# A layernorm, attention and mixture-of-experts layer on eight cores: resident Q/K weights with single buffers, in place of streamed Q/K weights with double buffers

## The chip, the cores and the metric

The kernel runs on all 8 cores of one Trainium2 chip (trn2). Every core runs the same program on its own share of the tokens, and no core talks to another. The time is the device time of the slowest core, in microseconds (us). Five engines work side by side in a core, each in the order of its own queue: PE (TensorE, matmuls and transposes), DVE (VectorE), ACT (ScalarE), POOL (GpSimd) and SP (SyncE). In this kernel POOL and SP do little but issue DMAs.

## The reference, cut to what matters

```python
x: (4, 8192, 1024) float32                     # each core: 4096 tokens = 2 segments of 2048
xn = layernorm(x)                              # no scale, no shift
# attention on every 4th token of a 2048-token segment: 512 tokens, 16 heads of 64, causal
xi = xn.reshape(4, 4, 2048, 1024)[:, :, 0::4, :]
q, k, v = split(xi @ w_in.T + b_in, 3)         # w_in (3072, 1024)
p = softmax(where(causal, q @ k.T / 8, -1e9));  o = (p @ v) @ w_out.T + b_out
attn = zeros_like(xn);  attn[:, :, 0::4, :] = o
# feed-forward on every token
shared = (silu(xn @ ws1) * (xn @ ws2)) @ ws3   # inner width 256
g = top-6-of-8 of softmax(xn @ wr), renormalised
routed = sum_e g[e] * ((silu(xn @ w1[e]) * (xn @ w2[e])) @ w3[e])   # inner width 128
out = x + attn + shared + routed
```

## The kernel before, in words

A core's 4096 tokens are two segments (`NSEG`), each of four groups r = 0..3 of 512 tokens (`NR`); group r holds the tokens whose index is r modulo 4, so only group 0 of a segment has attention. A group is four tiles q of 128 tokens. The program emits, in this order: layernorm of group (0,0), `attention(0)`, the weights still missing, `ffn_group` for (0,0) to (0,3), `attention(1)`, and `ffn_group` for (1,0) to (1,3). `em` puts a closure on the list of one engine with the semaphores it must wait for; an engine runs its list strictly in order, so the order of the emission is the order of the work.

**Weights.** They come from HBM as float32 and are cast to bf16 by DMAs of the POOL queue. The rows of `w_in` and `w_out` must be transposed: a chunk of 128 rows goes into one of the two slots of `WinNat`, PE transposes it in 8 steps into PSUM bank T0 or T1 (lines 210 and 286), DVE copies it to its place (lines 226 and 296). The DMA of a chunk waits until the transposes of the chunk two before it are done (`tr_read`). Chunks 0 to 7 are Q, 8 to 15 K, 16 to 23 V and 24 to 31 `w_out`. V and `w_out` are transposed once and stay. The Q and the K chunk of a pair of heads are streamed by `stream_qk(hp, buf)` one pair ahead, into the two buffers of `WqkS`, and again in the second segment: 32 streamed chunks in all. The router's, the shared and the expert weights are 21 plain DMAs. `witems` is the list of all resident weights in the order of loading; `wpump(2)` emits two items at the end of each head pair of the attention, `wensure(n)` all up to the nth.

**Attention.** `attention(seg)` loops over 8 pairs of heads, hp. For each pair: the transposes of the output of the pair before (`attn_pair_out`, line 650, copied to `OFM` in line 657), Q and K (`qkv_pair`, lines 464 and 482, 8 matmuls each), at hp 0 and 4 V for half of the heads (`v_batch`, line 508), the first scores (lines 531 and 534), probabilities times V of the pair before (`av_head`, lines 621 and 624), `Exp` on ACT (lines 546 and 551), the last scores (lines 563 and 566, the one of the odd head being the last matmul of the pair), `Exp` (lines 578 and 583), the causal masks on DVE (line 599), then `stream_qk` of the next pair, `wpump(2)` and `ln_pump()`. Q2, K2 and pT have two buffers, taken in turn by hp.

**Layernorm.** `ln_pre` takes one tile: load into one of two `XF` slots by the SP queue, sum on DVE (line 350), sum of squares on ACT (line 352), four small ACT operations and one on DVE, normalisation on DVE into a slot of `xn_tm` (line 372). `ln_tr` transposes the tile on PE (line 390) and DVE copies it to `XN` (line 399), which has a buffer for each of two groups. `ln_pump()` emits at most one `ln_tr` and one `ln_pre`; it is called once in every head pair, and in `ffn_group` once after the routing, once after the gate transposes and once after each of four pairs of experts. A tile of group r may be transposed only when the group two before it is finished. With four slots of `xn_tm` the `ln_pre` may be four tiles ahead of the `ln_tr`.

**Feed-forward.** `ffn_group(seg, r)`: router (line 723) and gates, shared projections (line 773), then the `tail` of the group before, then `HS` (lines 787 and 796), and for each of four pairs of experts 32 matmuls with W1 and W2 (line 829), `Silu` into `s1e` on ACT (line 847), three products on DVE (lines 851, 857, 862). `tail`: for each tile 2 x 10 matmuls (2 x 19 for group 0, with `Wo`; line 897), copies to one of two output slots on ACT (line 911), a DMA of the POOL queue that adds x to it (line 917), and the store on the SP queue (line 920). `HS`, `s1e` and the output slots `out_sb` have two buffers.

Of the kernel before, what the change touches and what calls it, by code (L numbers as in the profile page):

```python
# [8 lines left out]
F32 = mybir.dt.float32  # L9
BF16 = mybir.dt.bfloat16  # L10
# [21 lines left out]
def build_nc():  # L32
# [20 lines left out]
    with ctx:  # L53
        A = ctx.enter_context

        Wv = A(nc.sbuf_tensor("Wv", [P, CI, 1024], BF16))
# [9 lines left out]
        WqkS = A(nc.sbuf_tensor("WqkS", [P, 2, 2, CI, 128], BF16))  # L66
# [9 lines left out]
        xn_tm = A(nc.sbuf_tensor("xn_tm", [P, 4, C], BF16))  # L76
# [8 lines left out]
        Q2 = A(nc.sbuf_tensor("Q2", [P, 2, 512], BF16))  # L85
        K2 = A(nc.sbuf_tensor("K2", [P, 2, 512], BF16))
        Vsb = A(nc.sbuf_tensor("Vsb", [P, NQ, 512], BF16))
        pT = A(nc.sbuf_tensor("pT", [P, 2, 2, 1536], BF16))
# [101 lines left out]
        worder = [16, 17, 18, 19, 20, 21, 22, 23] + list(range(24, 32))  # L190
# [56 lines left out]
        for e in range(E):  # L247
# [7 lines left out]
        _chunks = [_mk_chunk_item(m) for m in worder[:8]]  # L255
        _wo = [_mk_chunk_item(m) for m in worder[8:]]
        witems = (_chunks[0:4] + _ffn_shared + _chunks[4:6] + _ffn_exp[0:4]
                  + _chunks[6:8] + _ffn_exp[4:8] + _ffn_exp[8:16] + _ffn_w3 + _wo)
# [8 lines left out]
        qk_ready = {}  # L267

        def stream_qk(hp, buf):
            for qk, m in ((0, hp), (1, 8 + hp)):  # L270
                def item(qk=qk, m=m):
                    mi = wmi[0]
                    wmi[0] += 1
                    sl = mi % 2
                    src_ = dwin[128 * m:128 * (m + 1), :]
                    em("gpsimd",
                       lambda g, sl=sl, src_=src_: g.dma_start(
                           out=WinNat[:, sl, :], in_=src_),
                       waits=[tr_read[sl]], inc="swin%d" % sl, k=16)
                    tb = "T%d" % sl  # L280

                    def mk_wtr(sl=sl, tb=tb):
                        def f(t):
                            ins = None
                            for ci in range(CI):
                                ins = t.transpose(bview[tb][:, ci, :],
                                                  WinNat[:, sl, 128 * ci:128 * (ci + 1)],
                                                  ident[:])
                            return ins
                        return f  # L290
                    tr = em("tensor", mk_wtr(),
                            waits=[("swin%d" % sl, 16 * (mi // 2 + 1)),
                                   ("sg", sg_done)] + bw(tb), inc="sp")
                    tr_read[sl] = ("sp", tr)
                    wqw = [("sp", tr)] + ([state["wqk_free"][buf]] if qk == 0 else [])
                    ev = em("vector", lambda v, tb=tb, buf=buf, qk=qk: v.tensor_copy(  # L296
                        WqkS[:, buf, qk], bview[tb][:, :, :]), waits=wqw, inc="sv")
                    bank[tb] = ("sv", ev)
                    qk_ready[(qk, buf)] = ev
                item()  # L300

# [11 lines left out]
        def wpump(n=2):  # L313
# [7 lines left out]
            "xntm_free": {0: None, 1: None, 2: None, 3: None},  # L321
# [100 lines left out]
        def can_pre(i):  # L422
            return i < len(lnq) and (i < 4 or lnp["tr"] >= i - 3)
# [33 lines left out]
        def qkv_pair(seg, hp):  # L457
            buf = hp % 2
            qb = hp % 2

            def mkq(hp=hp, buf=buf, qb=qb):
# [7 lines left out]
            cq = em("tensor", mkq(),  # L469
                    waits=[("sv", state["xn_ready"][(seg, 0)]),  # L470
                           ("sv", qk_ready[(0, buf)]),
                           ("sb", sb_done), ("sg", sg_done)] + bw("A0"), inc="sp")
            eq = em("scalar", lambda s, qb=qb: s.activation(out=Q2[:, qb, :],
                                                            in_=pA[:, 0, :],
                                                            func=AF.Identity),
                    waits=[("sp", cq), state["q2_free2"][qb]], inc="sa")
# [550 lines left out]
```

How the kernel before makes its waits and increments, by code:

```python
            def run(eng_obj, wt=wt, fn=fn, inc=inc, k=k):  # L139
                for s, v in wt:
                    eng_obj.wait_ge(S[s], v)
                ins = fn(eng_obj)
                if inc is not None:
                    ins.then_inc(S[inc], k)
```

## Time and profile before

| | us |
|---|---|
| median of two runs | 1003.77 (995.18 and 1012.36) |
| the profiled execution | 991.22 |
| its span on the slowest core, core 3 | 989.7 |
| spans of the eight cores | 975.8 to 989.7 |
| busy: PE, ACT, DVE, POOL | 753.8, 279.6, 274.1, 77.4 |

The span is the time from the first to the last instruction of the core; the profiled execution's own time is 1.5 us more. In the rows of a timeline the first number is the start in us from the start of the span, the second the time from the first start to the last end of the instructions of the row, then engine, line of the kernel, operation, output and inputs with their shapes and the count; what stands in brackets is how long the engine had been idle and what released it. "SPq" and "POOLq" are queues that issue DMAs. The clock column of a stretch is the granted clock of PE, 1.00 being 2.4 GHz.

### The profile page before, as it was taken

The numbers are of one execution on the slowest core, as the hardware profiler recorded it, in microseconds if no ns is written. First come the engines' busy times: TensorE is split into PE (matmuls) and PEld (weight loads), VectorE is DVE, ScalarE is ACT, GpSimd is POOL, SyncE is SP. The second block draws the span as 40 slices with busy tenths as digits, with TensorE's granted clock in tenths as the row PEclk, the third lists the DMA queues.
The fourth block names the chain that finished last, engine by engine and source line by source line (L and its number), as shares of the span: only waits on it lengthen the run. The fifth ranks groups of instructions, "written<-read, shape, count | busy, mean of one in ns | idle before, by whom it ended". The sixth has DMA issues, their size and how long they took to land.

```text
span 989.7 us, 12302 instructions; the slowest of 8 cores (975.8 to 989.7 us)
## 1 busy us (share of the span) xinstructions
PE 753.8 (76%) x4320; PEld 345.8 (35%) x4320; DVE 274.1 (28%) x580; ACT 279.6 (28%) x472; POOL 77.4 (8%) x117
## 2 busy tenths in 40 slices
PE   1386687329998687688687778889999688988983
PEld 1234433214443233243233235344443233433331
DVE  2414414313300440351152045233310350230220
ACT  1234234201101532351352254332112451211210
POOL 3111224010000001000000100000001000001001
PEclk9996678758999789799888887877999789998997
DMA  6365949940025105403511743110015303304206
GB/s 98 95 85 108 129 52 120 153 70 11 1 52 141 63 1 127 128 23 69 144 43 26 183 91 64 23 23 1 0 23 128 99 8 85 86 1 103 68 12 158
DMA packets 41930, 71.60 MB, mean 72 GB/s; under 512 B 20112, under 2 KB 22160, under 8 KB 41872
## 3 DMA queue, kind: packets, MB, share of 16 engines
q0 software_dynamic: 32656, 37.26, 26.4%
q1 hardware_dynamic: 9216, 33.56, 10.1%
q8 instruction: 38, 0.62, 0.3%
q14 instruction: 20, 0.16, 0.1%
HBM read 74.50 MB, written 16.78 MB: 92 GB/s over the span
## 4 chain that ended last, share of the span: by engine, by line
PE 52%; DMA 19%; ACT 10%; DVE 9%; issue 8%; POOL 1%; DVEq 0%; ACTq 0%; SPq 0%; POOLq 0%
PE pQ L897 8%; PE pA L829 7%; PE pK L897 6%; PE pB L829 6%; DMA osb<-x 6%; DMA WinNat<-w_out 5%; PE pA L464 4%; PE pA L773 4%; DMA out<-osb 3%; PE pA L482 3%; PE pB L773 3%; DMA WinNat<-w_in 3%; DMA XF<-x 2%; DVE HP L851 2%; DVE st_s L350 2%
## 5 line engine op out<-in xcount | busy, mean ns | idle before, releaser
L829 PE MATMUL pA<-XN,W 128*128 128x512 bf16 x512 | 126.9, 405 | 51.2 <-ACT s1e L847 39.3
L829 PE MATMUL pB<-XN,W 128*128 128x512 bf16 x512 | 115.7, 379 | 0.0
L829 PEld LDWEIGHTS pA<-XN,W 128*128 128x128 bf16 x512 | 50.5, 103 | 119.1 <-issue 72.2
L917 POOL DMA_DIRECT2D osb<-x x32 | 27.2, 849 | 640.2 <-ACT osb L911 634.5
L897 PE MATMUL pQ<-W,HP 128*128 128x512 bf16 x256 | 73.9, 441 | 0.0
L829 PEld LDWEIGHTS pB<-XN,W 128*128 128x128 bf16 x512 | 50.1, 98 | 60.4
L796 DVE TENSOR_TENSOR HS<-HS,pB 128x512 bf16<-128x512 bf16 x16 | 10.5, 684 | 216.7 <-ACT HS L787 206.9
L911 ACT ACTIVATE osb<-pQ 128x512 f32<-128x512 f32 x32 | 19.1, 597 | 177.7 <-PE pQ L897 132.3
L851 DVE TENSOR_TENSOR HP<-s1e,pB 128x1024 bf16<-128x1024 bf16 x32 | 39.1, 1221 | 107.5 <-PE pB L829 79.6
L847 ACT ACTIVATE s1e<-pA 128x1024 bf16<-128x1024 f32 x32 | 32.8, 1024 | 99.7 <-PE pA L829 99.5
L897 PE MATMUL pK<-W,HP 128*128 128x512 bf16 x256 | 60.9, 381 | 0.0
L210 PE MATMUL ptT<-ident,WinNat 128*128 128x128 bf16 x128 | 16.2, 306 | 56.9 <-DMA WinNat<-w_out 29.4
L352 ACT ACTIVATE xn_tm<-XF 128x1024 bf16<-128x1024 f32 x32 | 33.6, 1051 | 56.6 <-DMA XF<-x 41.6
L897 PE MATMUL pQ<-Ws,HS 128*128 128x512 bf16 x64 | 21.6, 423 | 35.9 <-ACT osb L911 28.4
L350 DVE TENSOR_REDUCE st_s<-XF 128x1 f32<-128x1024 f32 x32 | 38.7, 1209 | 33.8 <-DMA XF<-x 33.8
L599 DVE TENSOR_TENSOR pT<-pT,utri 128x128 bf16<-128x128 bf16 x128 | 20.2, 220 | 99.2 <-ACT pT L578 97.8
L464 PE MATMUL pA<-XN,WqkS 128*128 128x512 bf16 x128 | 44.8, 513 | 2.2 <-DVE WqkS L296 1.9
L390 PE MATMUL ptT<-ident,xn_tm 128*128 128x128 bf16 x256 | 24.1, 249 | 25.3 <-DVE xn_tm L372 17.7
L897 PEld LDWEIGHTS pQ<-W,HP 128*128 128x128 bf16 x256 | 28.1, 110 | 39.5 <-issue 16.3
L773 PE MATMUL pA<-XN,Ws 128*128 128x512 bf16 x128 | 40.6, 488 | 0.0
L372 DVE TENSOR_SCALAR xn_tm<-XF,st_m,st_r 128x1024 bf16<-128x1024 f32 x32 | 26.1, 817 | 43.1 <-ACT st_r L369 43.1
L897 PEld LDWEIGHTS pK<-W,HP 128*128 128x128 bf16 x256 | 25.4, 99 | 31.8 <-issue 2.8
(138 smaller groups left out, 946.6 us busy)
## 6 DMA issues: line engine op xcount, KB each, us to landing
XF<-x SPq DMA_DIRECT2D x32, 512.0 KB, 4.9
osb<-x POOLq DMA_DIRECT2D x32, 512.0 KB, 5.7
out<-osb SPq DMA_DIRECT2D x32, 512.0 KB, 3.1
WinNat<-w_in POOLq DMA_DIRECT2D x40, 256.0 KB, 4.7
W<-w POOLq DMA_DIRECT2D x16, 256.0 KB, 12.0
W<-w POOLq DMA_DIRECT2D x1, 2048.0 KB, 35.8
WinNat<-w_out POOLq DMA_DIRECT2D x8, 256.0 KB, 4.3
Ws<-ws POOLq DMA_DIRECT2D x3, 512.0 KB, 12.1
```

Source lines behind the costliest of these rows:

```text
L350: crs = em("vector", lambda v, seg=seg, j=j, gslot=gslot: v.reduce_sum(st_s[:, seg, j:j + 1], XF[:, gslot, :], axis=AX), waits=ldw, inc="sv")
L352: csq = em("scalar", lambda s, seg=seg, j=j, gslot=gslot, xsl=xsl: s.activation(out=xn_tm[:, xsl, :], in_=XF[:, gslot, :], func=AF.Square, ...
L372: cxn = em("vector", lambda v, seg=seg, j=j, gslot=gslot, xsl=xsl: v.tensor_scalar(out=xn_tm[:, xsl, :], in0=XF[:, gslot, :], scalar1=st_m ...
L390: ins = t.transpose(bview[tb][:, ci, :], xn_tm[:, xsl, 128 * ci:128 * (ci + 1)], ident[:])
L464: t.matmul(pA[:, 0, :], WqkS[:, buf, 0, ci, :], XN[:, 0, ci, :], start=(ci == 0), stop=False)
L482: t.matmul(pA[:, 1, :], WqkS[:, buf, 1, ci, :], XN[:, 0, ci, :], start=(ci == 0), stop=False)
L773: ins = t.matmul(bview[bn], Wsx[:, ci, 128 * k:128 * (k + 1)], XN[:, rb, ci, :], start=(ci == 0), stop=(ci == CI - 1))
L829: ins = t.matmul(bview[bn], Wx[:, e, ci, :], XN[:, rb, ci, :], start=(ci == 0), stop=(ci == CI - 1))
L847: cse = em("scalar", lambda s, epp=epp: s.activation(out=s1e[:, epp, :, :], in_=pA[:, :, :], func=AF.Silu), waits=[("sp", cw10), ("sp", cw ...
L851: cu = em("vector", lambda v, e0=e0, epp=epp: v.tensor_tensor(HP[:, e0:e0 + 2, :], s1e[:, epp, :, :], pB[:, :, :], op=ALU.mult), waits=[(" ...
L897: ins = t.matmul(bview[bn], lt, rh, start=(i == 0), stop=(i == len(ops) - 1))
L917: em("gpsimd", lambda g, seg=seg, r=r, q=q, sl2=sl2: g.dma_start(out=out_sb[:, sl2, :], in_=xv[seg, r, q], accum_op=ALU.add), waits=[("sa" ...
```

## The change

The Q and K weights become resident in `Wqk` (the 16 chunks are loaded and transposed once), and `stream_qk` and both of its calls ahead of segment work are gone. The list of weights has a new order, in which the chunks of the 8 pairs of heads stand between pairs of expert weights; `wpump(2)` is gone from the head loop, and `qkv_pair` itself calls `wensure` for its two chunks, ahead of its first matmul. `Q2`, `K2`, `pT`, `HS`, `s1e` go from two buffers to one, `xn_tm` from four slots to two, with `can_pre` letting `ln_pre` be two tiles ahead of `ln_tr` instead of four. The second output slot is now the memory of `WinNat`, read as float32. Shapes and number of all other operations stay.

```diff
-        WqkS = A(nc.sbuf_tensor("WqkS", [P, 2, 2, CI, 128], BF16))
+        Wqk = A(nc.sbuf_tensor("Wqk", [P, CI, 2048], BF16))
-        xn_tm = A(nc.sbuf_tensor("xn_tm", [P, 4, C], BF16))
+        xn_tm = A(nc.sbuf_tensor("xn_tm", [P, 2, C], BF16))
-        Q2 [P, 2, 512]; K2 [P, 2, 512]; pT [P, 2, 2, 1536]; HS and s1e [P, 2, 2, 512]; out_sb [P, 2, 1024]
+        Q2 [P, 512];    K2 [P, 512];    pT [P, 2, 1536];    HS and s1e [P, 2, 512];    out_sb [P, 1024]
...
-        worder = [16, 17, 18, 19, 20, 21, 22, 23] + list(range(24, 32))
+        worder = [0, 8, 16, 17, 18, 19, 1, 9, 2, 10, 3, 11, 20, 21, 22, 23,
+                  4, 12, 5, 13, 6, 14, 7, 15] + list(range(24, 32))
...
-        witems = (_chunks[0:4] + _ffn_shared + _chunks[4:6] + _ffn_exp[0:4]
-                  + _chunks[6:8] + _ffn_exp[4:8] + _ffn_exp[8:16] + _ffn_w3 + _wo)
+        witems = (_chunks[0:6] + _ffn_shared + _chunks[6:8] + _ffn_exp[0:2]
+                  + _chunks[8:10] + _ffn_exp[2:4] + _chunks[10:12] + _ffn_exp[4:6]
+                  + _chunks[12:16] + _ffn_exp[6:8] + _chunks[16:18] + _ffn_exp[8:10]
+                  + _chunks[18:20] + _ffn_exp[10:12] + _chunks[20:22] + _ffn_exp[12:14]
+                  + _chunks[22:24] + _ffn_exp[14:16] + _ffn_w3 + _wo)
...
-        def stream_qk(hp, buf):
...
-            xsl = state["tile"] % 4
+            xsl = state["tile"] % 2
...
         def can_pre(i):
-            return i < len(lnq) and (i < 4 or lnp["tr"] >= i - 3)
+            return i < len(lnq) and (i < 2 or lnp["tr"] >= i - 1)
...
         def qkv_pair(seg, hp):
-            buf = hp % 2
-            qb = hp % 2
+            wensure(max(widx[hp], widx[8 + hp]) + 1)
...
-                        t.matmul(pA[:, 0, :], WqkS[:, buf, 0, ci, :],
+                        t.matmul(pA[:, 0, :], Wqk[:, ci, 128 * hp:128 * (hp + 1)],
                                  XN[:, 0, ci, :], start=(ci == 0), stop=False)
...
-            ce = em("scalar", lambda s, pp=pp: s.activation(
-                out=pT[:, pp, 0, 0:1024].rearrange("p (a b) -> p a b", a=2, b=512),
+            ce = em("scalar", lambda s: s.activation(
+                out=pT[:, 0, 0:1024].rearrange("p (a b) -> p a b", a=2, b=512),
                 in_=pA[:, :, :], func=AF.Exp, bias=EXPB, scale=f32(0.125)),
-                waits=[("sp", cse_), state["pt_free2"].get((pp, 0))], inc="sa")
+                waits=[("sp", cse_), state["pt_free"][0]], inc="sa")
...
-            state["q2_free2"][qb] = ("sp", cso_)
-            state["k2_free2"][qb] = ("sp", cso_)
+            if hp is not None:
+                state["q2_free"] = ("sp", cso_)
+                state["k2_free"] = ("sp", cso_)
...
-            state["pt_free2"][(pp, pi)] = ("sp", cav)
+            state["pt_free"][pi] = ("sp", cav)
...
                 pend_av = (hp, cmk_e, cmk_o)
-                if hp < 7:
-                    stream_qk(hp + 1, (hp + 1) % 2)
-                wpump(2)
                 ln_pump()
...
-                          ([state["hs_free2"][gp_]] if k == 0 else []),
+                    waits=[("sp", ca[("a1", k)])] + ([state["hs_free"]] if k == 0 else []),
...
-                    waits=[("sp", cw10), ("sp", cw11), state["cu_par"][epp]], inc="sa")
+                    waits=[("sp", cw10), ("sp", cw11), last_chp2], inc="sa")
...
+                    oslot = (out_sb[:, :] if sl2 == 0 else
+                             WinNat[:, :, :].rearrange("p a b -> p (a b)").bitcast(F32))
...
+                            if sl2 == 1 and state["st_uses"][1] == 0:
+                                ew.append(tr_read[0])
+                                ew.append(tr_read[1])
...
-        wensure(4)
+        wensure(6)
         ensure_group(0, 0)
-        stream_qk(0, 0)
         attention(0)
...
-                if seg == 0 and r == NR - 1:
-                    stream_qk(0, 0)
```

## Rows read from the trace of the kernel before

**Rows 1.** The page: chain of waits that ended last, by engine, shares of the span

```profile
PE 52%; DMA 19%; ACT 10%; DVE 9%; issue 8%; POOL 1%; DVEq 0%; ACTq 0%; SPq 0%; POOLq 0%
```

**Rows 2.** Timeline, from the end of attention(0) to the first router

```profile
189.44 0.43 DVE L657 COPY OFM<-ptT 128x512 bf16<-128x512 bf16 x1 [0.84 <-PE ptT L650]
204.96 1.01 PE L210 MATMUL ptT<-ident,WinNat 128*128 128x128 bf16 x8 [15.63 <-DMA WinNat<-w_out]
...
226.89 1.04 PE L723 MATMUL pB<-Wr,XN 128*128 128x8 bf16 x32
```

**Rows 3.** Timeline, start-up: first streamed chunk load after V, to first Q

```profile
22.54 0.53 POOL L277 DMA_DIRECT2D WinNat<-w_in  x1 [2.34 <-PE ptT L210]
22.71 1.21 DVE L350 TENSOR_REDUCE st_s<-XF 128x1 f32<-128x1024 f32 x1
...
43.89 0.69 DVE L399 COPY XN<-ptT 128x1024 bf16<-128x1024 bf16 x1 [1.26 <-PE ptT L390]
...
46.90 2.99 PE L464 MATMUL pA<-XN,WqkS 128*128 128x512 bf16 x8 [0.30 <-DVE WqkS L296]
```

**Rows 4.** The page: issues of WinNat loads, KB each, median us to landing

```profile
WinNat<-w_in POOLq DMA_DIRECT2D x40, 256.0 KB, 4.7
```

**Rows 5.** Loads of XF, issue to landing, in the stretches 0:50 and 50:80

```profile
DMA to landing us min/median/max: 3.4/4.0/6.1
DMA to landing us min/median/max: 10.7/10.7/10.7
```

**Rows 6.** Timeline of PE and DVE between head pairs 1 and 2, segment 0

```profile
76.23 0.21 PE L566 MATMUL pB<-Q,K 64*128 64x128 bf16 x1
80.51 3.27 PE L464 MATMUL pA<-XN,WqkS 128*128 128x512 bf16 x8
...
76.63 1.30 DVE L599 TENSOR_TENSOR pT<-pT,utri 128x128 bf16<-128x128 bf16 x8 [0.50 <-ACT pT L578]
77.85 1.28 DVE L296 COPY WqkS<-ptT 128x1024 bf16<-128x1024 bf16 x2
79.05 1.21 DVE L350 TENSOR_REDUCE st_s<-XF 128x1 f32<-128x1024 f32 x1
...
81.81 0.81 DVE L372 TENSOR_SCALAR xn_tm<-XF,st_m,st_r 128x1024 bf16<-128x1024 f32 x1 [0.70 <-ACT st_r L369]
```

**Rows 7.** Timeline of PE between head pairs 2 and 3, segment 0

```profile
90.03 0.21 PE L566 MATMUL pB<-Q,K 64*128 64x128 bf16 x1
...
100.80 3.37 PE L464 MATMUL pA<-XN,WqkS 128*128 128x512 bf16 x8
```

**Rows 8.** Timeline, head pair 3 of segment 1: Exp, and end of the even AV

```profile
610.20 1.02 ACT L546 ACTIVATE pT<-pA 128x1024 bf16<-128x1024 f32 x1 [0.89 <-PE pA L534]
610.97 0.18 DVE L632 RECIPROCAL rz<-pQ 128x4 f32<-128x4 f32 x1 [3.57 <-PE pQ L624]
```

**Rows 9.** Timeline of PE between head pairs, segment 1, first and last of seven

```profile
573.55 0.21 PE L566 MATMUL pB<-Q,K 64*128 64x128 bf16 x1
577.41 3.62 PE L464 MATMUL pA<-XN,WqkS 128*128 128x512 bf16 x8
...
659.72 0.21 PE L566 MATMUL pB<-Q,K 64*128 64x128 bf16 x1
...
662.62 1.69 PE L464 MATMUL pA<-XN,WqkS 128*128 128x512 bf16 x5
```

**Rows 10.** Timeline of the expert loop, groups (1,1) and (1,2)

```profile
763.81 3.61 PE L829 MATMUL pA<-XN,W 128*128 128x512 bf16 x16 [1.88 <-ACT HS L787]
774.75 1.22 DVE L350 TENSOR_REDUCE st_s<-XF 128x1 f32<-128x1024 f32 x1 [8.71 <-DMA XF<-x]
791.75 3.62 PE L829 MATMUL pA<-XN,W 128*128 128x512 bf16 x16
849.27 3.61 PE L829 MATMUL pA<-XN,W 128*128 128x512 bf16 x16 [1.88 <-ACT HS L787]
865.25 3.62 PE L829 MATMUL pA<-XN,W 128*128 128x512 bf16 x16
```

More of the change, by code:

```diff
@@ L266, in build_nc @@
                     widx[m] = pos
-        qk_ready = {}
-        def stream_qk(hp, buf):
[L270 to L300, printed above, removed]
         swfa_done = 16 * 4
@@ L469, in qkv_pair, with mkk @@
             cq = em("tensor", mkq(),
-                    waits=[("sv", state["xn_ready"][(seg, 0)]),
-                           ("sv", qk_ready[(0, buf)]),
+                    waits=[("sv", state["xn_ready"][(seg, 0)]), ("sv", wch_ready[hp]),
                            ("sb", sb_done), ("sg", sg_done)] + bw("A0"), inc="sp")
[L473 to L476, printed above, removed]
+            eq = em("scalar", lambda s: s.activation(out=Q2[:], in_=pA[:, 0, :],
+                                                     func=AF.Identity),
+                    waits=[("sp", cq), state["q2_free"]], inc="sa")
             bank["A0"] = ("sa", eq)
-            def mkk(hp=hp, buf=buf):
+            def mkk(hp=hp):
                 def f(t):
                     for ci in range(CI):
-                        t.matmul(pA[:, 1, :], WqkS[:, buf, 1, ci, :],
+                        t.matmul(pA[:, 1, :],
+                                 Wqk[:, ci, 1024 + 128 * hp:1024 + 128 * (hp + 1)],
                                  XN[:, 0, ci, :], start=(ci == 0), stop=False)
@@ L526, in scores_c01 @@
         def scores_c01(seg, hp, eq, ek):
-            qb = hp % 2
             def mk(base, pX):
                 def f(t):
-                    t.matmul(pX[:, 0, 0:512], K2[base:base + 64, qb, 0:128],
-                             Q2[base:base + 64, qb, 0:512], start=True, stop=True,
+                    t.matmul(pX[:, 0, 0:512], K2[base:base + 64, 0:128],
+                             Q2[base:base + 64, 0:512], start=True, stop=True,
                              tile_position=(base, 0))
-                    return t.matmul(pX[:, 1, 0:384], K2[base:base + 64, qb, 128:256],
-                                    Q2[base:base + 64, qb, 128:512], start=True,
-                                    stop=True, tile_position=(base, 0))
+                    return t.matmul(pX[:, 1, 0:384], K2[base:base + 64, 128:256],
+                                    Q2[base:base + 64, 128:512], start=True, stop=True,
+                                    tile_position=(base, 0))
                 return f
@@ L786, in ffn_group @@
                 bn = "A%d" % k
-                cs_[k] = em("scalar", lambda s, k=k, gp_=gp_: s.activation(
-                    out=HS[:, gp_, k, :], in_=pA[:, k, :], func=AF.Silu),
-                    waits=[("sp", ca[("a1", k)])] +
-                          ([state["hs_free2"][gp_]] if k == 0 else []),
+                cs_[k] = em("scalar", lambda s, k=k: s.activation(
+                    out=HS[:, k, :], in_=pA[:, k, :], func=AF.Silu),
+                    waits=[("sp", ca[("a1", k)])] + ([state["hs_free"]] if k == 0 else []),
                     inc="sa")
@@ L868, in ffn_group, with tail @@
                 ln_pump()
-            def tail(seg=seg, r=r, chp_last=chp_last, ch=ch, gp_=gp_):
+            def tail(seg=seg, r=r, chp_last=chp_last, ch=ch):
                 fin_last = None
```

104 lines of the change are left out of this document (44 added, 60 removed).

## The prediction, made before the changed kernel was run

> **What bounds the kernel now.** I read the chain of waits first, then the timeline at the stage borders, since the change touches each stage in another way. PE carries 52% of the chain and DMA 19% [rows 1]; no engine is busy throughout, so a change of order counts only where it lengthens or shortens the path of PE. Three places matter. At the end of `attention(0)` the last copy is over at 189.44 + 0.43 = 189.87, and PE then sits 15.6 us until the first `w_out` chunk lands at 204.96; from there eight chunks, two at a time in `WinNat`, take 21.9 us up to the router at 226.89 [rows 2]. In the head loop PE is idle between the last scores of one pair and Q of the next, because transposes of two chunks and their DVE copies lie there [rows 6, 9]. In the expert loop a group with `ln_pre` in it is far slower than one without [rows 10]. I split the span at the first router and go through four terms.
>
> **Start-up.** `wensure(6)` puts six chunks ahead of the layernorm, where there were four, and DVE copies them in order ahead of the first sum. The load that was the second streamed one, issued at 22.54 [rows 3], is now the sixth. With 4.7 us to land [rows 4] and about 2 us for eight transposes (1.01 in [rows 2]), a copy of this size (0.69 in [rows 3]) and the signals, DVE comes to the first sum at about 29.3, not 22.71 [rows 3]: +6.6. The four tiles follow as before and end at 44.58 before [rows 3], so at 51.2; the two Q/K transposes that then took until 46.90 are already done, which gives back 2.2. Net +4.4. The router's and shared weights and two experts, which POOL used to issue from 47 us on, now come right behind the chunks at about 23 us, beside the loads of tiles 2 and 3. A load of `XF` took 4.0 us with little beside it and 10.7 us among weight loads [rows 5]; a tile lasts (44.58 - 22.71) / 4 = 5.5, and the load of tile 2 starts when tile 0 is normalised (3.6 after its sum), so it has 2 x 5.5 - 3.6 = 7.4 us before anyone waits; I add 10.7 - 7.4 = 3.3. The Trainium skill (DMA: Bandwidth & Descriptors, section on queues, rings and completion order) says that a DMA engine takes packets from its queue rows in turn, which agrees with 4.0 against 10.7; without that sharing the addition would be nothing. Start-up: **+7.7**, bounds +4.4 and +11 (both loads late).
>
> **Attention of segment 0.** First the order on DVE. In [rows 6] the masks end at 77.93, the two Q/K copies follow at once (77.85, 0.6 each), and only then the layernorm: sum at 79.05, normalisation over at 82.62, a chain of 3.57 us that waits for ACT twice. The change calls `ln_pump` first and emits the chunks in the next `qkv_pair`. So the Q copy is queued behind that chain, behind the copy of the transposed tile (0.7) and of `OFM` (0.4), and the chunk's transposes need a T bank that one of these two frees. From the start of the last scores matmul to Q: masks end +1.7, chain +3.6, two copies +1.0, transposes +1.0, Q copy +0.7 = 8.0, against 80.51 - 76.23 = 4.28 [rows 6]: +3.7. By the same sum, with what each gap holds: pair 1 +3.2 (nothing transposed in it), 2 +3.7, 5 +3.7, 6 +2.7, and 7 +0.8 (no `ln_pre` in it any more). Between pairs 2 and 3 the gap was 100.80 - 90.03 = 10.77 [rows 7], since two V chunks were loaded and waited for there; now 8.0: -2.8. In pair 4 all four V chunks come together: two wait for a slot, so another 4.7 us landing after the first transposes; with the old wait there as well I get +0.8, and +1.4 because chunks 4 and 12 are transposed between V and Q. Sum +13.5.
>
> Second, **the one pT**. `Exp` of a pair's first scores must now wait for AV of the pair before, which PE does right after these scores. In [rows 8] `Exp` starts at 610.20 and the reciprocal that waits for the even AV at 610.97: 0.75 us later at each pair but 0 and 4, where AV is done earlier. Six pairs: +4.5. The odd half waits for nothing new, as ACT is busy with the even half (1.02) until the odd AV is over.
>
> Start-up, order and pT make +25.7 at the last scores. Then the cover counts. No `ln_pre` stands before the last AV any more (about -2.4, the part of its 3.6 us that was beside nothing, an estimate), and the 15.6 us of waiting for `w_out` [rows 2] shrinks: two experts and W3 are left behind the last Q/K chunk instead of eight and W3, so `w_out` should be there when PE is. 25.7 - 2.4 - 15.6 = +7.7 at the first router; the 21.9 us of the eight chunks stay. Segment 0: **+7.7**. If that cover were gone (`w_out` as late behind PE as before), it would be +23.3.
>
> **FFN of segment 0**: nothing. The five pumps per group emit the same number of `ln_tr` and `ln_pre`. A single `HS` waits for the last matmul of the tail, which ACT has already waited for in order to copy the tail's last tile. `Silu` into the single `s1e` waits for the product before, and that starts when W1's matmuls do, 3.6 us [rows 10] before `Silu` can. Q2 and K2 are written after matmuls that stand on PE behind their last readers. The second output slot is as free as before.
>
> **Attention of segment 1.** The 14 transposed chunks in the loop and their copies are gone (the two of pair 0 stood in idle time of group (0,3), an estimate), and so are 16 loads of POOL's queue, for which nobody waited. From the start of the last scores matmul to the next Q, or V at pair 4, seven gaps: the first 577.41 - 573.55 = 3.86, the last 662.62 - 659.72 = 2.90 [rows 9], 25.3 in all. What remains is the last matmul (0.2), `ln_tr` in four of them (0.8, from the 1.01 of eight transposes in [rows 2]), the output transposes, half as many, in six, and in pair 4 the masks ahead of AV (3.0 in all): 8.9. That is -16.4. The one pT costs 6 x 0.75 = 4.5 again: **-11.9**. Bounds: the first Q group runs at either 3.62 or 1.9 us (3.62 in [rows 9], the 1.2 GHz level at first), and more idle PE may make all seven slow (+4) or none (-7).
>
> **FFN of segment 1.** With two slots of `xn_tm`, `ln_pre` runs two tiles ahead, not four. Counting the pumps through the program, two of its calls leave `attention(0)` (pairs 6 and 7) and come back in group (1,2), which had none. Group (1,1) shows what they do: its second group of experts after the first two pumps starts at 791.75, 27.94 after 763.81; in (1,2) it is 865.25 - 849.27 = 15.98 [rows 10]. The difference is the load of `XF` queued on SP behind the store of the tail's last tile, for which DVE waits 8.71, then the chain and two switches of ACT's table. **+12.0**, bound from below by 2.6 (if the load had landed).
>
> **Sum.** 991.2 + 7.7 - 11.9 + 12.0 = 999.0, against the profiled execution's own 991.22. The two other times are 995.18 and 1012.36, the median 12.5 above the profile. I take the nearer one's distance, 4, and say **1003**. A measurement of this kernel tells 2% (20 us) from no change.
>
> **Rivals.**
> (a) *Faster, the weights come in time and little stands in their way.* The DVE order costs nothing (Q copies slip in before the chain because it ends early) and XF is not slowed: segment 0 is +4.4 + 4.5 - 6.5 (the gap of [rows 7] falls to the 4.28 of [rows 6]) + 2.2 - 18.0 = -13.4, in all 991.2 - 13.4 - 11.9 + 12.0 = 978, or 966 if the load of group (1,2) is hidden too. For it speaks the 15.6 us hole; against it that DVE is strictly in order and the chain waits for ACT twice [rows 6]. 0.22, of which 0.08 beyond 2%.
> (b) *Slower, chunks late behind experts.* In the head loop every Q/K pair now has two expert loads ahead of it in POOL's queue. I expect them to be through in the 90.03 - 76.23 = 13.8 us of a pair [rows 6, 7]. If not, a gap like that of [rows 7] opens ahead of pairs 1, 2, 5, 6 and 7 as well, 10.77 - 4.28 = 6.5 each, +32.5 in place of the 11.3 that I have for the six gaps: +21. In all 999.0 + 21 = 1020, 1024 with the same 4. It decides once two experts and two chunks take longer to land than a pair lasts. `XF` at 10.7 [rows 5] speaks for it, the 4.7 of chunks [rows 4] against. 0.23.
> (c) *Every lost second buffer costs.* ACT, DVE and PE wait for each other in each expert pair. The Trainium skill (Trainium Kernel Development and Optimization, Best Practices) says to double-buffer for performance, which speaks against this change as a whole. Priced by rows: if `Silu` (1.02, the size of [rows 8]) no longer ran beside matmuls in 32 expert pairs, +33, 1036. Against it: 3.6 us of matmuls lie between. 0.05.
> The forecast has 0.50.
>
> **Chances and range.** Faster than 2% 0.09, slower 0.25 ((c), most of (b)), within 0.66. Lower end from (a) 979, upper from (b) 1025.
>
> **What would show it.** First Q matmul at 51 to 55 us; Q/K copies (now line 226) after the normalisation in segment 0; `Exp` released by AV; no long wait of line 210 for `w_out`; router at 235; in segment 1 no transposes of `WinNat`, gaps near 1 us; group (1,2) about 84 us instead of 72. The prediction is wrong if PE waits for a DMA in each head pair, or if segment 0 ends before 227.

## The result and the profile after

The changed kernel takes **1017.81 us** (median of 11 runs, 1005.33 to 1077.06) against 995.29 (10 runs, 986.21 to 1012.36) for the kernel before on the same chip: ratio **1.0218 [1.017, 1.0267]**, slower, though the interval leaves open whether by more than 2%. The prediction said 1003, a change within 2%; 1018 lies inside its range, but its likeliest case was the wrong one. In some executions of either kernel one die is disturbed (its cores show a lower granted clock and are some per cent longer), so ratios leave these out (of e10_wout two of four), and as the profiled execution of the changed kernel is one of them (cores 4, 6 and 7, up to 1020.2), its rows below are from core 3, whose die was not.

This table carries the comparison. A stage runs from one first matmul to the next; the prediction's terms stand beside what was measured. The times are medians over the eight cores, and where a stage has several pieces (gaps, runs, groups) the sum of their medians; so the stages need not add up to the last line: they make +19.9 together, the last matmul moves by +16.0, and on cores 0 to 3 alone it moves by +13.2. The failed term does not hang on this: in e6 and e7 below, whose later head pairs are those of the changed kernel, segment 0 takes 160.3 and 159.7 and the seven gaps 74.6 and 73.2. Group (1,2) does in part: in e1, e2, e4, e5 and e6 it takes 81.2 to 81.8, not 82.7.

| stage (median of 8 cores, us) | before | after | measured | predicted |
|---|---|---|---|---|
| start to first Q | 46.5 | 54.0 | +7.5 | +7.7 |
| segment 0, first Q to last scores | 131.9 | 159.9 | **+28.0** | +18.0 |
| of it the 7 gaps between pairs | 50.7 | 73.3 | +22.6 | +13.5 |
| of it the 8 runs Q to last scores | 81.5 | 86.1 | +4.6 | +4.5 |
| last scores to first router | 43.1 | 26.7 | -16.4 | -18.0 |
| FFN (0,0) to (0,3), together | 330.7 | 330.3 | -0.4 | 0 |
| segment 1, first Q to last scores | 115.3 | 106.6 | -8.7 | -11.9 |
| of it the 7 gaps | 33.9 | 17.6 | -16.3 | -16.4 |
| of it the 8 runs | 80.8 | 89.1 | +8.3 | +4.5 |
| groups (1,0), (1,1) | 135.2 | 132.4 | -2.8 | 0 |
| group (1,2) | 70.9 | 82.7 | +11.8 | +12.0 |
| group (1,3) and tail | 96.1 | 96.9 | +0.8 | 0 |
| end of the last matmul | 975.1 | 991.1 | **+16.0** | +7.8 |

The page of the changed kernel (the page is that of the slowest core, here core 4), chain of waits by engine, answers [rows 1]; then the queue that loads the weights and adds x to the output (37.26 MB before).

```profile
PE 52%; DMA 18%; ACT 12%; DVE 8%; issue 7%; POOL 1%; DVEq 0%; ACTq 0%; SPq 0%; POOLq 0%
q0 software_dynamic: 30352, 33.06, 23.3%
```

The weights that are no longer streamed are 4.2 MB less, and the share of DMA in the chain hardly changes: what was saved in traffic did not shorten the path.

**Start-up**, changed kernel, core 3, timeline; it answers [rows 3]. Then `XF` loads in the stretches 0:28 and 28:50, which answer [rows 5].

```profile
27.34 1.21 DVE L315 TENSOR_REDUCE st_s<-XF 128x1 f32<-128x1024 f32 x1
...
42.33 1.22 DVE L315 TENSOR_REDUCE st_s<-XF 128x1 f32<-128x1024 f32 x1 [4.01 <-DMA XF<-x]
...
53.67 2.72 PE L427 MATMUL pA<-XN,Wqk 128*128 128x512 bf16 x6 [1.16 <-DVE XN L364]
```

```profile
DMA to landing us min/median/max: 3.7/4.3/4.9
DMA to landing us min/median/max: 5.4/9.9/11.2
```

The first sum is 4.6 us later than before (22.71; forecast 6.6), and a later load of `XF` makes DVE wait 4.0 us beside the weight loads (forecast 3.3). The Trainium skill (DMA: Bandwidth & Descriptors, section on queues, rings and completion order) says that a DMA engine takes packets from its queue rows in turn; 9.9 us (the middle one of three loads) with both queues loaded against 4.3 agrees with it.

**A gap of segment 0**, pair 1 to 2, changed kernel, core 3, PE and DVE; it answers [rows 6].

```profile
89.38 0.21 PE L520 MATMUL pB<-Q,K 64*128 64x128 bf16 x1
...
89.79 1.30 DVE L552 TENSOR_TENSOR pT<-pT,utri 128x128 bf16<-128x128 bf16 x8 [1.26 <-ACT pT L532]
91.01 1.21 DVE L315 TENSOR_REDUCE st_s<-XF 128x1 f32<-128x1024 f32 x1
...
93.77 0.81 DVE L337 TENSOR_SCALAR xn_tm<-XF,st_m,st_r 128x1024 bf16<-128x1024 f32 x1 [0.70 <-ACT st_r L334]
94.50 0.68 DVE L364 COPY XN<-ptT 128x1024 bf16<-128x1024 bf16 x1
95.09 0.41 DVE L609 COPY OFM<-ptT 128x512 bf16<-128x512 bf16 x1
95.66 1.87 PE L211 MATMUL ptT<-ident,WinNat 128*128 128x128 bf16 x16 [4.88 <-DVE OFM L609]
96.77 0.69 DVE L227 COPY Wqk<-ptT 128x1024 bf16<-128x1024 bf16 x1 [1.26 <-PE ptT L211]
97.93 2.26 PE L427 MATMUL pA<-XN,Wqk 128*128 128x512 bf16 x5 [0.41 <-DVE Wqk L227]
```

From 89.38 to 97.93 are 8.55 us, where it was 4.28. Read DVE down the column: masks, the whole layernorm chain, two copies, and only then the chunk's copy. PE sits idle for 4.88 us until the copy of `OFM` frees the bank for the transposes. No wait for a DMA is in the gap: the chunks had landed.

**The gap at pair 4**, changed kernel, core 3, PE with one row of POOL.

```profile
127.32 0.28 PE L520 MATMUL pB<-Q,K 64*128 64x128 bf16 x1
...
133.67 1.87 PE L211 MATMUL ptT<-ident,WinNat 128*128 128x128 bf16 x16 [3.10 <-DVE rz L584]
...
135.22 0.53 POOL L203 DMA_DIRECT2D WinNat<-w_in  x1 [17.98 <-PE ptT L211]
...
140.52 1.01 PE L211 MATMUL ptT<-ident,WinNat 128*128 128x128 bf16 x8 [4.99 <-DMA WinNat<-w_in]
142.65 1.01 PE L211 MATMUL ptT<-ident,WinNat 128*128 128x128 bf16 x8 [1.12 <-DVE Wv L227]
144.93 3.30 PE L467 MATMUL pA<-Wv,XN 128*128 128x512 bf16 x8 [1.26 <-DVE Wv L227]
...
154.92 1.07 PE L211 MATMUL ptT<-ident,WinNat 128*128 128x128 bf16 x16
156.81 1.89 PE L427 MATMUL pA<-XN,Wqk 128*128 128x512 bf16 x8 [0.81 <-DVE Wqk L227]
```

Two V chunks are in the slots and may be transposed only at 133.67; the other two are issued at 135.22, when a slot is free, and PE waits 4.99 us for them.

**The one pT**, head pair 2 of segment 1, changed kernel, core 3; it answers [rows 8], which are of pair 3.

```profile
606.22 0.37 PE L488 MATMUL pA<-Q,K 64*128 64x512 bf16 x1 [0.95 <-ACT K L451]
...
607.61 1.02 ACT L502 ACTIVATE pT<-pA 128x1024 bf16<-128x1024 f32 x1 [1.65 <-PE pQ L576]
```

`Exp` is now released by line 576, the sums of the AV before, and starts 1.39 us after the first scores; the median over the cores is 1.39 to 1.41 in all six pairs (1 to 3 and 5 to 7) of either segment, where it was 0.63.

**Group (1,2)**, changed kernel, core 3: SP's queue, DVE's first sum, PE on the experts. It answers the (1,2) half of [rows 10].

```profile
853.13 0.33 SPq L869 DMA_DIRECT2D out<-WinNat  x1
853.62 1.08 SPq L312 DMA_DIRECT2D XF<-x  x2
858.18 1.22 DVE L315 TENSOR_REDUCE st_s<-XF 128x1 f32<-128x1024 f32 x1 [6.84 <-DMA XF<-x]
864.60 5.29 PE L776 MATMUL pA<-XN,W 128*128 128x512 bf16 x16 [7.35 <-ACT s1e L793]
```

The load of `XF` leaves SP only behind the store of the tail's last tile; DVE waits 6.84 us for it, and PE 7.35 us for the `Silu`, which stands on ACT behind the layernorm operations of the same tile and two table loads of 1.28 us each.

**The end of attention(0)**, changed kernel, core 3; it answers [rows 2].

```profile
219.19 0.43 DVE L609 COPY OFM<-ptT 128x512 bf16<-128x512 bf16 x1 [0.84 <-PE ptT L602]
219.77 1.87 PE L211 MATMUL ptT<-ident,WinNat 128*128 128x128 bf16 x16 [0.68 <-DVE OFM L609]
...
240.45 1.04 PE L671 MATMUL pB<-Wr,XN 128*128 128x8 bf16 x32
```

The 15.6 us wait for `w_out` is gone, and the 20.7 us of its eight chunks remain.

### The profile page after: what moved, and what is told of

It reads as the page before. It is cut to its first block, busy times and chain, and to the rows that moved or that the text cites. A ratio compares the mean times of both kernels' runs of the same rounds, so it can differ in the third digit from the quotient of the medians.

```text
span 1020.2 us, 11868 instructions; the slowest of 8 cores (991.5 to 1020.2 us)
## 1 busy us (share of the span) xinstructions
PE 741.3 (73%) x4126; PEld 338.5 (33%) x4192; DVE 264.8 (26%) x564; ACT 285.0 (28%) x476; POOL 68.8 (7%) x101
## 4 chain that ended last, share of the span: by engine, by line
PE 52%; DMA 18%; ACT 12%; DVE 8%; issue 7%; POOL 1%; DVEq 0%; ACTq 0%; SPq 0%; POOLq 0%
PE pA L776 8%; PE pQ L843 7%; PE pB L776 6%; PE pK L843 6%; PE pA L427 4%; DMA osb<-x 4%; PE pA L721 4%; DMA XF<-x 4%; DMA WinNat<-x 3%; DMA out<-osb 3%; PE pA L443 3%; PE pB L721 3%; DVE st_s L315 3%; DMA WinNat<-w_in 2%; PE ptT L211 2%
## 5 line engine op out<-in xcount | busy, mean ns | idle before, releaser
L776 PEld LDWEIGHTS pA<-XN,W 128*128 128x128 bf16 x512 | 50.7, 103 | 133.1 <-issue 86.7
L211 PE MATMUL ptT<-ident,WinNat 128*128 128x128 bf16 x256 | 30.0, 300 | 66.7 <-DMA WinNat<-w_in 28.2
L797 DVE TENSOR_TENSOR HP<-s1e,pB 128x1024 bf16<-128x1024 bf16 x32 | 39.1, 1221 | 100.4 <-PE pB L776 73.2
L866 POOL DMA_DIRECT2D osb<-x x16 | 13.5, 843 | 655.0 <-ACT osb L860 655.0
L427 PE MATMUL pA<-XN,Wqk 128*128 128x512 bf16 x116 | 44.4, 546 | 11.7 <-DVE Wqk L227 8.8
L211 PEld LDWEIGHTS ptT<-ident,WinNat 128*128 128x128 bf16 x256 | 24.4, 137 | 71.6 <-issue 71.6
L860 ACT ACTIVATE osb<-pQ 128x512 f32<-128x512 f32 x16 | 9.6, 597 | 135.2 <-PE pQ L843 83.8
L843 PEld LDWEIGHTS pQ<-W,HP 128*128 128x128 bf16 x256 | 28.2, 110 | 40.1 <-issue 17.3
```

What stands on the lines that cost most here:

```text
L211: ins = t.transpose(bview[tb][:, ci, :], WinNat[:, sl, 128 * ci:128 * (ci + 1)], ident[:])
L427: t.matmul(pA[:, 0, :], Wqk[:, ci, 128 * hp:128 * (hp + 1)], XN[:, 0, ci, :], start=(ci == 0), stop=False)
L776: ins = t.matmul(bview[bn], Wx[:, e, ci, :], XN[:, rb, ci, :], start=(ci == 0), stop=(ci == CI - 1))
L797: cu = em("vector", lambda v, e0=e0: v.tensor_tensor(HP[:, e0:e0 + 2, :], s1e[:, :, :], pB[:, :, :], op=ALU.mult), waits=[("sa", cse), ("s ...
L843: ins = t.matmul(bview[bn], lt, rh, start=(i == 0), stop=(i == len(ops) - 1))
```

## The experiments

All are timed against the kernel before. "Saves" is the difference of a ratio to the 1.0218 of the changed kernel, times 995; it carries the intervals of both ratios, 6 to 9 us together. The last matmul of the median core, 991.1 in the changed kernel, is at 979.9 in e1, 972.8 in e2, 987.0 in e3, 994.3 in e4, 956.0 in e5, 979.3 in e6 and 952.1 in e7. Theory: three mechanisms inside the changed kernel (order on DVE, V chunks of pair 4, one pT) and the depth of `xn_tm` cost what it lost. Rival: the single buffers taken together, or the loads themselves.

**e1_pt2**, a second pT in memory of `HP`:

```diff
+        pT1 = HP[:, 0:6, :].rearrange("p (a b) c -> p a (b c)", a=2, b=3)
+            pt = pT if hp % 2 == 0 else pT1
-                waits=[("sp", cse_), state["pt_free"][0]], inc="sa")
+                waits=[("sp", cse_), state["pt_free2"].get((hp % 2, 0))], inc="sa")
```

> The changed kernel with the second pT buffer back (in the memory of HP, which is idle in the attention). Theory A (the loss is a sum of order costs on DVE, the one pT, the start-up and the layernorm tiles moved to group (1,2)): from the first Q to the last scores each of 12 head pairs becomes about 1.0 us shorter, 6 in each segment, so Exp (line 502 of the changed kernel) starts before AV is over; 12 us less in all, ratio to the kernel before 1.010. Theory B (chunks come late by DMA, the pairs are bound by loads): segment 1 gains 6, segment 0 nothing, 1.016. Theory C (all single buffers cost alike): 5 us or less from this one, 1.017.

Measured 1003.99, 1.0063 [1.0025, 1.0102]: it saves 15 us. Segment 0 falls from 159.9 to 154.3, segment 1 from 106.6 to 99.5, together 12.7 where the prediction had 9.0. In its timeline (core 3, head pair 1 of segment 1) the release is that of [rows 8] again:

```profile
592.14 0.37 PE L490 MATMUL pA<-Q,K 64*128 64x512 bf16 x1 [0.94 <-ACT K L453]
592.77 1.02 ACT L505 ACTIVATE HP<-pA 128x1024 bf16<-128x1024 f32 x1 [0.88 <-PE pA L493]
```

0.63 us after the first scores instead of 1.39, in all twelve pairs: the 0.75 us of the prediction is right for `Exp`, 9.1 us in all. The last scores do not add to it: they start 1.17 us behind that `Exp` in the changed kernel and in e1 (1.36 and 1.22 in two of its pairs). The other 3.6 of the 12.7 us lie elsewhere, 1.7 between Q's first matmul and the first scores (1.5 of it in segment 1) and the rest in the gaps. What changed ahead of the scores is the pace of the Q and K matmuls: the 8 matmuls of Q take 3.62 or 1.90 us at the two levels of the granted clock, and in pair 2 of segment 1 the median from Q to the first scores is 5.30 us before, 6.28 after the change and 5.63 in e1.

**e2_chunks_first**, the two Q/K chunks of the next pair put ahead of the layernorm step again:

```diff
+                if seg == 0 and hp in (0, 1, 2, 4, 5, 6):
+                    wensure(max(widx[hp + 1], widx[9 + hp]) + 1)
                 ln_pump()
```

> The changed kernel with the two chunks of the next head pair emitted before ln_pump, at pairs 0, 1, 2, 4, 5 and 6 of segment 0, as stream_qk did. Theory A: the gaps from the last scores to Q, 6.4, 8.6, 8.6, 8.9, 6.8, 4.6 us after the change, fall to the 2.9, 4.3, 4.3, 4.4, 3.6, 2.9 of the kernel before, 21 us in all; part may come back as a wait for w_out; router of group (0,0) 15 to 21 us earlier, ratio 1.001 to 1.007. Theory B: the chunks are late by their DMA whatever DVE does, so the gaps stay within 1 us, 1.02. Theory C: nothing, 1.02.

Measured 997.78, 0.9961 [0.9915, 1.0007]: the added lines save 26 us, 18.3 at the last matmul of the median core. The seven gaps are 2.9, 4.4, 4.4, 29.8, 4.3, 3.7 and 3.0 against 6.6, 8.6, 8.6, 29.3, 8.8, 6.8 and 4.6. In the gap of pair 1 to 2 (core 3) the copies are ahead of the sum:

```profile
86.23 0.21 PE L520 MATMUL pB<-Q,K 64*128 64x128 bf16 x1
...
87.85 1.28 DVE L227 COPY Wqk<-ptT 128x1024 bf16<-128x1024 bf16 x2
...
89.05 1.21 DVE L315 TENSOR_REDUCE st_s<-XF 128x1 f32<-128x1024 f32 x1
...
90.51 3.33 PE L427 MATMUL pA<-XN,Wqk 128*128 128x512 bf16 x8
```

No gap but that of pair 4 waits for the DMA of a chunk, here or in the changed kernel. That refutes rival (b) of the prediction.

**e3_xn4**, four slots of `xn_tm`, as before the change, with the bias rows of Q, K and V not loaded, to make room:

```diff
-            xsl = state["tile"] % 2
+            xsl = state["tile"] % 4
-            return i < len(lnq) and (i < 2 or lnp["tr"] >= i - 1)
+            return i < len(lnq) and (i < 4 or lnp["tr"] >= i - 3)
```

> The changed kernel with four slots of xn_tm and ln_pre up to four tiles ahead; room for it is made by one row of 1024 for the four bias vectors, all zero here, so the text of the biases of Q, K and V is left out. Theory A: group (1,2) falls from 80 to 71 us and nothing else in segment 1 moves; segment 0 gains nothing, its head pairs 6 and 7 get their ln_pre back and grow by 0 to 5 us; ratio 1.010 to 1.015. Theory C: other groups gain too, more than 15 us in all, below 1.007.

Measured 1013.59, 1.0146 [1.0068, 1.0224]: it saves about 7 us, not 12, and the interval reaches to 1.0218. Group (1,2) is 71.1 again (from 82.7), so that term is confirmed; but the gap ahead of pair 7 grows from 4.6 to 8.1 and the stretch to the router from 26.7 to 29.2, as the two layernorm steps come back to pairs 6 and 7. The two slots had taken some cost out of segment 0.

**e4_rest2**, all other lost second buffers given back (Q2, K2, `HS`, `s1e`, an output slot of its own), in memory of `HP` and `Vsb`; for the output slot this kernel too leaves out the bias rows:

```diff
+        Q2s = [Q2, HP[:, 0, :]]
+        K2s = [K2, HP[:, 1, :]]
+        HSs = [HS, Vsb[:, 0:2, :]]
+        s1es = [s1e, Vsb[:, 2:4, :]]
+        out_sb2 = A(nc.sbuf_tensor("osb2", [P, 1024], F32))
```

> The changed kernel with second buffers for Q2, K2, HS and s1e (in memory that is idle in the stage) and with an output slot of its own in place of WinNat's; the bias vectors share one row of zeros for it. Theory A: none of the four is waited for, no stage moves by more than 1 us, ratio 1.02. Theory C (a single buffer costs wherever there were two): 10 us or more, 1.01 or less. A third possibility, that DMAs into WinNat's memory are slower than into the slot before: the tails of groups get 1 to 3 us shorter each, 10 us in all.

Measured 1018.17, 1.0217 [1.016, 1.0274], and no stage moves by more than 1.5 us: attention 1 takes 106.7, group (1,2) 81.2. Five of the halved buffers cost nothing that can be seen together, within the 0.6% of the interval. Rival (c) holds for pT and `xn_tm` alone.

**e5_vmid**, e2 for all pairs, and the middle V chunks early: slots for chunks 20 to 23 in the memory of `out_sb`, transposed in pairs 1 and 2:

```diff
-        worder = [0, 8, 16, 17, 18, 19, 1, 9, 2, 10, 3, 11, 20, 21, 22, 23,
+        worder = [0, 8, 16, 17, 18, 19, 1, 9, 20, 21, 2, 10, 22, 23, 3, 11,
+                if seg == 0 and hp in (1, 2):
+                    wensure(widx[19 + 2 * hp] + 1)
```

> The run e2_chunks_first with one thing more: V chunks 20 to 23 get two slots of their own (the memory of the first output slot, idle then) and are transposed in head pairs 1 and 2 while ACT is at Exp, and pair 3 too emits its chunks ahead of ln_pump. Theory A, with the part that was mis-sized (pair 4, where four V chunks and two Q/K chunks pass through two slots): the gap ahead of pair 4 falls from 29.8 us to 13.3, what it is in segment 1 without any chunk; pairs 1 and 2 grow by at most 1 us each; ratio 0.9961 - 0.015 = 0.981, less if w_out becomes the bound (then a wait for it of up to 10 us appears ahead of the first router). If the gap is bound by something else in pair 4 (AV, V matmuls), it stays above 20 us.

Measured 978.7, 0.9789 [0.973, 0.9848]: 43 us better than the changed kernel and 2.1% faster than the kernel before. Segment 0 takes 126.0; the gap at pair 4 falls from 29.3 to 16.0, the seven together from 73.3 to 38.4. The 13.3 us of pair 4 have two parts: from the last scores to V 17.3 falls to 6.0, by the early V chunks, and from V to Q 12.0 to 10.0, as chunks 4 and 12 are no longer transposed between them. At pair 4 (core 3) V follows without a chunk of its own:

```profile
113.30 0.31 PE L525 MATMUL pB<-Q,K 64*128 64x128 bf16 x1
113.54 1.89 PE L216 MATMUL ptT<-ident,WinNat 128*128 128x128 bf16 x16
...
119.33 1.01 PE L472 MATMUL pA<-Wv,XN 128*128 128x512 bf16 x2
...
129.34 1.90 PE L432 MATMUL pA<-XN,Wqk 128*128 128x512 bf16 x8
...
141.91 3.62 PE L432 MATMUL pA<-XN,Wqk 128*128 128x512 bf16 x8
```

**e6_start**, only the first Q and K chunk ahead of the layernorm, and one V chunk behind each of its four tiles:

```diff
-        wensure(6)
-        ensure_group(0, 0)
+        wensure(2)
+        for i_ in range(NQ):
...
+            wensure(3 + i_)
```

> The changed kernel with two chunks ahead of the layernorm of group (0,0) and one chunk behind each of its four tiles, instead of six ahead. Theory A (DVE copies chunks in order ahead of the first sum, and weight loads slow the loads of XF): the first Q starts at 41 to 45 us instead of 54, all else as in the changed kernel, ratio 1.009 to 1.013. Rival (the start is bound by the loads of x alone): stays above 50, 1.02.

Measured 1002.19, 1.0065 [1.0033, 1.0098]: it saves 15 us. The first Q is at 40.4, not 54.0, and nothing later gives it back. The kernel before, at 46.5, had 6 us of this loss too.

**e7_prefetch**, the load of `XF` for tile + 2 emitted at the end of `ln_pre(tile)`, when its slot is read for the last time:

```diff
+            if tile + 2 < NSEG * NT:
+                xf_load(tile + 2)
```

> The changed kernel with the load of XF for the tile two ahead issued right behind the ln_pre that frees its slot, so that it no longer stands behind the stores of the next tail on SP's queue. Theory A (the first ln_pre of a group waits for a load that is late only by its place in the queue): group (1,2) falls from 82 to about 74 us, (0,1), (0,2), (0,3) and (1,1) by 8 each, 40 us in all, ratio 0.98. Rival (the cost of ln_pre in a group is its work on DVE and ACT and the table switches): at most 2 us per group, above 1.012.

Measured 969.59, 0.9748 [0.9701, 0.9794]: it saves 47 us, the most of any single edit. Groups (0,1), (0,2), (0,3), (1,1), (1,2) take 83.9, 76.2, 104.2, 84.0, 75.8 against 92.8, 84.5, 112.7, 91.8, 82.7. In group (1,2), core 3:

```profile
815.95 1.28 DVE L753 TENSOR_TENSOR HS<-HS,pB 128x512 bf16<-128x512 bf16 x2 [31.61 <-ACT HS L745]
...
818.08 1.20 DVE L323 TENSOR_REDUCE st_s<-XF 128x1 f32<-128x1024 f32 x1
...
824.48 3.61 PE L786 MATMUL pA<-XN,W 128*128 128x512 bf16 x16 [0.41 <-ACT s1e L803]
```

The sum waits for no DMA, and PE waits 0.41 us instead of 7.35 at the second expert pair.

**e8_before_pt1**, the kernel before with one pT (`pp = hp % 2` becomes `pp = 0` in four places):

> The kernel before with one thing of the change alone: one pT in place of two. Measured so far the other way round: 5.6 us in segment 0 and 7.1 in segment 1 came back with the second one. Theory A: 10 to 13 us slower in all, but what segment 0 loses (5 us) is hidden behind the wait for w_out, so 5 to 7 us at the end of the span, ratio 1.005 to 1.008. If the cost is not hidden there: 1.012.

Measured 1011.27, 1.0133 [1.008, 1.0186], +13 us. The runs Q to last scores go from 81.5 to 89.1 and from 80.8 to 87.1: the edit costs here about what its reverse, e1, gave back there. Of these 13.9 us 9.1 are the release (0.63 to 1.39 in twelve pairs again). That the hole ahead of `w_out` would hide segment 0's part was wrong: that stretch falls only from 43.1 to 40.6 while segment 0 grows by 8.2. The hole comes along with the pairs, and the traces show why. The first two `w_out` chunks are not issued late but land late: here the issues of `WinNat<-w_out` with their time to landing, core 3, kernel before (stretch 155:205) and e8 (155:206).

```profile
WinNat<-w_out POOLq DMA_DIRECT2D x2, 256.0 KB, 32.9
WinNat<-w_out POOLq DMA_DIRECT2D x2, 256.0 KB, 31.8
```

They are issued at 168.4 (median) before and 174.0 in e8, when the chunks of pair 7 are transposed, and land 32 us later in both, behind the eight expert loads and the 2 MB of W3 that POOL issues just ahead of them. In the changed kernel they are issued at 203.6 and land 13 us later.

**e9_all**, e1, e5, e6 and e7 together:

> The changed kernel with four repairs at once: second pT, chunks ahead of ln_pump and V chunks in slots of their own, one chunk behind each tile at the start, loads of XF issued early. Theory A (the costs are separate terms of the path of PE, so they add): ratio 1.0218 - 0.0155 - 0.043 - 0.0153 - 0.047 = 0.901; if DMA becomes the bound at the end of attention(0), a wait of 5 to 15 us for weights appears between the last scores and the first router (26.4 us in the changed kernel) and it is 0.906 to 0.916. Rival (the same idle time was counted several times): above 0.93.

Measured 913.27, 0.9181 [0.9114, 0.9248]. Of the last matmul's 991.1 the four parts alone take off 12.7, 33.9, 13.6 and 39.0 (the last three from segment 0's stage, the start and the end), 99.2 in all; together it ends at 895.5, 95.6 earlier. At the last matmul they add within 4%. The measured time adds less: the four ratios forecast 0.901, and 0.9181 is above that and above the 0.916 of its other branch, whose wait for weights ahead of the router did not appear either (27.1). So 103 us were gained of 120. Most of the difference lies in the distance of the slowest core behind the median one, 11.4 in the changed kernel and 6.4, 4.4, 12.3 and 4.7 in e1, e5, e6 and e7: e1, e5 and e7 each take 5 to 7 us off it, and e9, at 6.7, only once.

**e10_wout**, e9 with the `w_out` chunks loaded into the output slot and transposed in pairs 3 to 6, and with W3 ahead of the last experts in the list of loads; the list is left out here:

```diff
-                if seg == 0 and hp in (1, 2):
+                if seg == 0 and hp in (1, 2, 3, 4, 5, 6):
                     wensure(widx[19 + 2 * hp] + 1)
```

> The run e9_all with the eight w_out chunks transposed in head pairs 3 to 6, in the two slots of V, W3 loaded ahead of the last experts. The 22 us that eight chunks take two at a time behind attention(0) should fall to 4 to 8 us between last scores and first router, against 2 to 6 us more in the head pairs: ratio 0.015 to 0.02 below e9_all. If the loads (about 133 us of DMA time up to the first router in the kernel before) are the bound there, pairs 3 to 7 wait for chunks and the gain is under 0.005.

Ratio 0.9049 [0.8906, 0.9193]; the profiled execution took 901.07. Last scores to router falls from e9's 27.1 to 4.3, but the start grows by 3.2 and segment 0 by 8.5 (120.8 to 129.3). The 16 DMA engines are 80 to 100% busy in most of the first seven slices, so the loads are likely the bound there; no run tested it. The DMA line of its page, in fortieths of the span:

```profile
DMA  8899989100152144226226120000053134006026
```

This version has the lowest ratio, but its interval and that of e9 overlap.

**e11_before_prefetch**, the kernel before with e7's edit:

> The kernel before with the loads of XF issued early, as in e7_prefetch. Theory A: groups (0,1), (0,2), (0,3) and (1,1) get 8 us shorter each, (1,2) has no ln_pre and stays at 71; ratio 0.965 to 0.97. The two ln_pre that the change moves to (1,2) then cost 75.8 - 71 = 5 us and not 11. And if the spread between cores (975.8 to 989.7 before, over 20 us after the change) comes from loads queued behind stores, it is below 8 us here too. Rival: no gain here, because the kernel before has its layernorm tiles further ahead; 0.99 or more.

Measured 962.97, 0.9674 [0.9588, 0.9761]. The same edit helps the kernel before by 3.3%; its spans lie 13.8 apart (947.9 to 961.7), not under 8 as expected. With the loads early on both sides the change costs 0.9748 - 0.9674 = 0.7% instead of 2.2%, which the two intervals do not tell from nothing; at the last matmul of the median core it costs 952.1 - 941.5 = 10.6 us instead of 16.0. Its group (1,2) costs 75.8 - 70.8 = 5.0 us instead of 11.8.

## Why the prediction was wrong

**The step that failed** is the first of segment 0, the order on DVE, "Sum +13.5": it measures +22.6. The seven gaps were forecast at +3.2, +3.7, -2.8, +2.2, +3.7, +2.7, +0.8 and came out at +3.7, +4.3, -2.4, **+7.7**, +4.4, +3.1, +1.7. So the mechanism was right gap by gap, 0.4 to 0.9 short each, and pair 4 alone makes 5.5 of the 9.1 missing. There I took over the old wait and added 0.8: from the last scores to V it measures +6.1 (11.3 to 17.3), while V to Q is right, +1.6 against +1.4. The rows at pair 4 show more: the first two V chunks are transposed 6.3 us after the last scores, behind layernorm and AV results, so the second two are requested only at 135.22, and on core 3 V begins 17.6 us after the last scores. e2 and e5 separate the two parts: chunks first gives back 20.9 us of gaps and leaves pair 4 (29.8), V early gives back 11.3 of the 13.3 at pair 4.

**The one pT** was priced right: 9.0 forecast (twice 4.5), 9.1 measured, 0.76 us at each of twelve pairs. What came with it was not priced: e1 gives back 12.7 in all, e8 costs 13.4 at the last matmul. In the changed kernel the runs of segment 1 grew by 8.3, and 4.6 of it is the release; 3.7 lies between Q's first matmul and the first scores. That is the bound of the prediction, "more idle PE may make all seven slow (+4)", which it kept out of the sum; what the clock did before each of these groups was not tested. The last pair holds most: on core 3 its Q group runs at a granted clock of 0.50 (the row below), and K follows 4.08 us behind Q's first matmul; before, the granted clock there was 0.82 and it was 2.59 us (662.62 in [rows 9]).

```profile
664.70 3.62 PE L427 MATMUL pA<-XN,Wqk 128*128 128x512 bf16 x8
```

**The base.** The sum was made on the profiled 991.22 plus 4, and 1003 was then held against the 1003.77 of two executions; ten gave 995.29. The prediction's own terms made +7.8. The last matmul of the median core moved by 16.0, the measured time by 22.5. What remains, about 6, lies in how far the slowest core is behind the median one, for which the prediction had no term: over the executions that the ratios use, the span of the slowest core less that of the median one is 5.9 us before (32 executions) and 11.4 after (8). It is 4.7 in e7, 6.4 in e1 and 6.7 in e9, but 12.3 in e6 and 7.2 in e11; why the cores drift apart stays open.

**Right:** start-up +7.5 (+7.7 forecast), by luck in part, since on core 3 the two further chunks cost 4.6 and not 6.6 us and the late load of `XF` 4.0 and not 3.3; the hole ahead of `w_out`, -16.4 (-18.0); the gaps of segment 1, -16.3 (-16.4); group (1,2), +11.8 (+12.0; 10.3 to 10.9 in e1, e2, e4, e5 and e6), by the load behind the store, which e3 and e7 remove in two ways; the FFN of segment 0 and the single `HS`, `s1e`, Q2 and K2 at nothing (e4). The router came at 240.45 on core 3, not at 235, by the failed term. Neither of the two signs that the prediction named for being wrong appeared, a wait for a DMA in each head pair or segment 0 ending before 227: the term failed in size, at one pair.

**The rivals.** (a) was wrong: DVE does not let the copies in. (b), slower by late chunks, gave 1020 to 1024, near the time measured, and yet its mechanism is absent: no gap but that of pair 4 waits for a DMA. (c) is wrong as a whole by e4. The Trainium skill (Trainium Kernel Development and Optimization, Best Practices) says to double-buffer for performance, to overlap DMA with compute. The runs agree for two of the seven buffers, pT (9.1 us of waits, 12.7 in all) and `xn_tm`, neither of which a DMA fills or reads, and not for the other five together (1.0217 against 1.0218), of which DMAs touch only the output slot.

## What to carry to other kernels

Before emission order is changed, write down the in-order queue of the engine that frees the bank, and price the whole chain that comes to stand ahead of the copy: a 3.6 us chain there was worth 3.1 to 4.4 us in each of four pairs, and the order alone gave back 2.6%. Where more loads come together than there are slots, price the wait for the second pair of them too: at pair 4 it was the step that failed. A load belongs where its slot becomes free, not where its data is needed, above all where it shares a queue with stores that wait. Halve a buffer only after asking who writes next and who read last: most second buffers here were worth nothing, and the one whose last reader stands right ahead of the next writer was worth 0.76 us of wait per use.

## What the runs showed of the hardware

A load of 512 KB took 4.3 us to land with few others and 9.9 us (the middle one of three, up to 11.2) beside weight loads; a load of 256 KB issued on POOL's queue behind eight others and one of 2 MB took 32 us. The eight-matmul Q group took 3.62 us at the lower of the two TensorE clock levels and 1.90 at the upper, in the same kernel (e5: 141.91 with a granted clock of 0.50, and 129.34 with 1.00), the faster one following V's matmuls without idle time and the slower one following a gap. The mean granted clock rose with the gaps closed, from 0.863 on core 3 of the changed kernel to 0.876 in e7 and 0.907 in e10:

```profile
core 3: 999.4 us, clock 0.863
```

```profile
core 3: 959.7 us, clock 0.876
```

```profile
core 3: 895.5 us, clock 0.907
```
